# The second key block weighed with the third and fourth, a group later: two runs of 32-column matmuls a group instead of three

## What is computed

```python
x = x + 0.5 * ffn(layernorm(x))
x = x + attention(layernorm(x))
x = x + 0.5 * ffn(layernorm(x))

# attention, per sequence and head
q = x @ Wq;  latent = x @ Wkv_down            # latent: 32 channels
k = latent @ Wk_up;  v = latent @ Wv_up
p = softmax(where(causal, q @ k.T / 8, -inf))
y = p @ v;  out = y @ Wout                    # summed over the heads
```

## Time and profile before

| | us |
|---|---|
| runs | 913.27, 915.11, 913.05 |
| median | 913.27 |
| span of the profiled execution | 915.6 |
| TensorE matmul busy | 858.2 (94%) |
| GpSimd busy | 731.9 (80%) |
| VectorE busy | 644.4 (70%) |
| ScalarE busy | 549.3 (60%) |
| weight loads (beside the matmuls) | 572.1 (62%) |
| matmuls of L755, blocks 1 to 3 | 110.1, 1536 records |
| matmuls of L755, block 0 | 69.3, 512 records |

### The profile page before, as it was taken

The page is one execution under the profiler, slowest core; times in us unless marked ns, Lnnn a source line. Parts: engine busy times, 40 slices in busy tenths (PEclk is TensorE's granted clock), DMA queues, the critical chain, the costliest instruction groups (busy, mean ns, idle before and its releaser), DMA issues. The chain is left out here.

```text
span 915.6 us, 21654 instructions
## 1 busy us (share of the span) xinstructions
PE 858.2 (94%) x7750; PEld 572.1 (62%) x7750; DVE 644.4 (70%) x1818; ACT 549.3 (60%) x1113; POOL 731.9 (80%) x834
## 2 busy tenths in 40 slices
PE   5688999999999999999999999999999999999886
PEld 4455666666576666666566666666666666657455
DVE  3387577678767677768767777876867767776645
ACT  4444666757666565756756665766656575655551
POOL 4304789898989989898898989898988989789732
PEclk9878999999999999999999999999999999999999
DMA  4446251523535151533535152443525153340000
GB/s 101 113 111 140 54 118 36 124 73 85 124 82 126 42 129 39 120 88 82 126 71 130 33 126 57 98 110 82 125 58 119 37 117 74 83 102 14 14 24 12
DMA packets 77546, 77.89 MB, mean 85 GB/s; under 512 B 9392, under 2 KB 51136, under 8 KB 77440
## 3 DMA queue, kind: packets, MB, share of 16 engines
q1 hardware_dynamic: 76640, 75.45, 35.5%
q10 hardware_dynamic: 800, 1.07, 0.4%
HBM read 9.90 MB, written 8.39 MB: 20 GB/s over the span
## 5 line engine op out<-in xcount | busy, mean ns | idle before, releaser
L483 POOL TENSOR_TENSOR first_probs<-first_probs,later_probs 128x768 f32<-128x768 f32 x240 | 371.2, 1555 | 23.7 <-PE bank L755 23.7
L593 ACT ACTIVATE later_probs<-bank 128x384 f32<-128x384 f32 (+1 forms) x448 | 231.0, 538 | 153.5 <-PE bank L742 152.5
L742 PE MATMUL bank<-q_stack,keys 123*128 123x512 f32 (+1 forms) x704 | 308.4, 463 | 9.8 <-ACT first_probs L593 8.3
L1059 DVE TENSOR_REDUCE maxima<-bank 128x1 f32<-128x512 f32 (+1 forms) x384 | 254.9, 682 | 67.5 <-PE bank L811 67.3
L811 PE MATMUL bank<-keys,q_stack 122*128 122x512 f32 (+3 forms) x1024 | 256.3, 338 | 11.6 <-issue 2.8
L811 PEld LDWEIGHTS bank<-keys,q_stack 122*128 122x128 f32 x1024 | 181.8, 193 | 103.0 <-issue 41.4
L593 ACT ACTIVATE first_probs<-bank 128x512 f32<-128x512 f32 x256 | 139.9, 594 | 106.1 <-PE bank L742 102.2
L1059 DVE TENSOR_REDUCE block_max<-bank 128x4 f32<-128x512 f32 x256 | 173.6, 678 | 39.8 <-PE bank L811 39.1
L742 PEld LDWEIGHTS bank<-q_stack,keys 123*128 123x128 f32 x704 | 127.9, 191 | 72.0 <-ACT first_probs L593 33.7
L516 POOL TENSOR_SCALAR_AFFINE_SELECT later_probs<-later_probs 128x512 f32<-128x512 f32 x192 | 124.1, 647 | 55.5 <-ACT later_probs L593 55.5
L755 PE MATMUL bank<-later_probs,lat 128*32 128x384 f32 (+2 forms) x1536 | 110.1, 389 | 0.7 <-POOL later_probs L516 0.7
(11 more groups left out here) (127 smaller groups left out, 831.2 us busy)
## 6 DMA issues: line engine op xcount, KB each, us to landing
q_stack<-q_high SPq DMA_DIRECT2D x256, 128.0 KB, 2.4
q_stack<-q_low SPq DMA_DIRECT2D x128, 128.0 KB, 2.5
out_dram<-x SPq DMA_DIRECT2D x32, 256.0 KB, 2.6
x_in<-in_L_attn_x_bld_dram SPq DMA_DIRECT2D x16, 256.0 KB, 3.2
x_back<-out_dram SPq DMA_DIRECT2D x16, 256.0 KB, 3.0
keys<-keys_staged SPq DMA_DIRECT2D x15, 192.0 KB, 2.5
keys<-keys_staged SPq DMA_DIRECT2D x30, 96.0 KB, 2.4
lat<-lat_staged SPq DMA_DIRECT2D x16, 64.0 KB, 1.9
```

Of the source, the lines that this page charges most:

```text
L483: nc.gpsimd.tensor_tensor(total, total, later_probs[j - 1][:, heads], ALU.add).then_inc(added, 1)
L593: nc.scalar.activation(probs_of(s)[:, e:e + heads, 0:n], score_bank(t, u)[:, 0:heads * n].rearrange("p (e q) -> p e q", e=heads), ACT.Exp) ...
L742: nc.tensor.matmul(score_bank(t, u)[:, 0:heads * n], keys[par][:, PLAIN_BLOCK[j], :], q_stack[par][:, first:first + heads, j * P:L], start ...
L1059: nc.vector.tensor_reduce(out, seg, AX.X, ALU.max).then_inc(a_free, 1)
```

## The change

In a step with s % 4 = 1 the second block (j = 1) of the last group is weighed first, then the third and fourth; the step with s % 4 = 3 weighs nothing. Between its exponentials and its weighing a second block now lives until the next group's second block is being made, so `later_probs` for j = 1 gets a second buffer, chosen by the group's parity, and the exponential that writes it waits for the weighing and the sums of two groups ago instead of one. The order in which blocks are weighed stays. The last sequence keeps its tables. The number of matmuls, exponentials, masks and sums is the same.

```diff
-WEIGH = [[], [3, 2], [2], [2]]
+WEIGH = [[], [4, 3, 2], [2], []]
@@
-        later_probs = [sb(f"later_probs{j}", [P, HG, L - P * j]) for j in range(1, TT)]
+        later_probs = [[sb(f"later_probs{j}{i}", [P, HG, L - P * j]) for i in range(2 if j == 1 else 1)]
+                       for j in range(1, TT)]
@@
-            return later_probs[s % TT - 1] if s % TT else first_probs[s // TT % 2]
+            g, j = divmod(s, TT)
+            bufs = later_probs[j - 1] if j else first_probs
+            return bufs[g % len(bufs)]
@@
-                    nc.gpsimd.tensor_tensor(total, total, later_probs[j - 1][:, heads], ALU.add).then_inc(added, 1)
+                    nc.gpsimd.tensor_tensor(total, total, probs_of(g * TT + j)[:, heads], ALU.add).then_inc(added, 1)
@@
                     if e == 0:
-                        wait_batch(act, pv_done, t, 0, STEPS, s - TT + 1)
+                        ago = 2 if j == 1 else 1
+                        wait_batch(act, pv_done, t, 0, STEPS, s - ago * TT + 1)
                         if j in ADDED:
                             wait_batch(act, added, t, 0, PARTS * G * len(ADDED),
-                                       PARTS * ((g - 1) * len(ADDED) + ADDED.index(j) + 1))
+                                       PARTS * ((g - ago) * len(ADDED) + ADDED.index(j) + 1))
```

More of the change, by code:

```diff
@@ L1077, in last_adds @@
                             total = first_probs[g % 2][:, heads, j * P:L]
-                            nc.vector.tensor_tensor(total, total, later_probs[j - 1][:, heads], ALU.add).then_inc(added, 1)
+                            nc.vector.tensor_tensor(total, total, probs_of(g * TT + j)[:, heads], ALU.add).then_inc(added, 1)
                 def next_statistics():
```

## The result

The changed kernel takes 936.82 us (median of 4 runs, 936.49 to 937.52), the kernel before 914.19 in the same comparison (4 runs). The ratio is 1.0242, 95% interval 1.0217 to 1.0266: 22.6 us slower. The forecast was 934.4, in a range of 923 to 939.

The account below looks back on a forecast made before the run. TensorE sets the pace except where GpSimd's chain holds the projection and ScalarE covers savings. +1.52 us in thirteen rounds (+19.8), +0.67 and +0.7 in sequences 0 and 14 sum to +21.2: 934.4 us, range 923 to 939.

Parts of the forecast that it names:

- The two prices: TensorE's cost of weighing a second block: 0.88 us alone, 0.65 us beside the third and fourth blocks.
- Steps 3, 5 and 7: Two runs taken and one 0.65 us addition before the projection, hidden by GpSimd's chain: gain 0.
- The distance: From the score of step 2 to the first projection, ended by GpSimd's y_norm: fixed at 15.13 us.
- Steps 9, 13 and 1: Places where TensorE's longer run adds 0.65 us each, claimed to be paid whole.
- Step 11: Run removed before the front's query matmul, which waits for ScalarE's copy: only 0.26 of 0.88 us comes off.
- Step 15: Run removed before step 0, whose first exponential waits behind ScalarE's four tiles: gain 0.17 us; TensorE's wait about 1.1.
- third rival: One ScalarE cover, in step 11 or 15, gives way: 0.62 or 0.71 us a sequence back, about 926 us; chance 0.11.
- Sequence 0: First sequence, with no projection or tail before it, so steps 7 and 11 are gained: +0.67 us.
- Sequence 14: Sequence with no front beside it: bounded by -0.9 and +1.5 us, taken as +0.7.
- fourth rival: Step 5's longer run delays GpSimd: up to 0.65 us more in 13 sequences, 943 us; chance 0.06.
- TensorE's pace everywhere: Second rival: TensorE sets the pace all the way, each removed run worth 0.23 us, 899.5 us; chance 0.08.
- Both rivals with a cover giving way: ScalarE's covers in steps 11 and 15: one gives way, about 926 us, chance 0.11; both, some 917, chance 0.04.

Follow-up runs that it names:

- m1: Kernel before with one max unit a sequence taken out of step 10 and one more put into step 6; ratio 1.0052 over the kernel before.
- m3: Changed kernel with two more max units in steps 6 and 7, two in step 11, fewer in steps 12 to 14; ratio 1.0179 over the kernel before.

## Why the prediction was right

**The two prices.** 0.65 in company and 0.88 alone: the run of step 1 grew by 0.65, and the run of step 7 was worth 0.87. 60 x 0.23 = 13.8 us of work would go away by that; TensorE's busy time, whose ends are modelled, shows 9.9.

**Steps 3, 5 and 7 give nothing.** The distance is 15.14, forecast unchanged at 15.13. The wait before the projection grew to 0.70, forecast 0.6. The experiments with the cut sum show that the cause is GpSimd, not a coincidence. The slack that I claimed for step 5's longer run is there, 0.65 where I had 0.79; nothing was put between the exponential's end and the mask's start. One part is right without its reason. I wrote that steps 3 and 7 together take 0.88 + 0.88 and that TensorE arrives 0.88 - 0.65 = 0.23 earlier, which counts only one of the two; with both it would be 1.11 earlier, and the wait about 1.5. For sequence 0 I called step 3 hidden without saying behind what. The rows of step 4 give the reason: step 3's saving ends there, at VectorE's reduction and ScalarE's tiles, and TensorE's last max unit before the projection comes 13.81 us after the score of step 2 instead of 14.03, 0.22 earlier. The time doesn't depend on it.

**Steps 9, 13 and 1 are paid whole,** but for 0.05 of step 9's, which step 10 takes back. Group 1 moved alone costs 0.60 a round, with nothing gained at step 7.

**Step 11.** Forecast 0.26 off; 0.17 came at the query matmul, which starts 0.14 after the copy's end where I had allowed 0.05, and 0.20 at the score behind it. Its wait is 0.55, forecast 0.7. **Step 15.** Forecast 0.17 off; alone it leaves 0.65 - 0.47 = 0.18. The number is right, and ScalarE's tiles do end last there, as the cut shows. But of the 0.88 VectorE took the first 0.44, which the forecast didn't have, and so the sign named for it, a wait of 1.1, failed: it is 0.71. So the third rival's price of 0.71 for a cover that gives way here was too high: by the rows 0.26 would have come back, and the cut tiles gave 0.24.

**The round.** +1.52 forecast, +1.51 measured. Counted from the score of step 2 on, the changed kernel's scores are behind by 0.65 from the middle of step 5, by 0.01 at the projection, by 0.65 in step 9, 0.60 in step 11, 0.40 in step 12, 1.05 from step 13, 0.85 in step 1 of the next sequence and 1.50 at its end: each term in its place.

**The ends.** Sequence 0, given +0.67, has it: from the first score of the attention to the first projection the profiles take 71.46 us before and 72.08 after, +0.62. Sequence 14, given +0.7, costs about twice that, 1.3: I took a gain before its projection, which has no wait for GpSimd in the kernel before, but in the changed one step 5's 0.65 brought TensorE and GpSimd there later by 0.3 (13.98 us from the score of step 2, then 14.32). That is the fourth rival's path, in this one sequence. On the other side the profile of before holds two single delays, 0.85 in the first of the rounds of the earlier trace rows, by the wait for the keys, and 0.33 in the round of 52.30 us that ends at 721.24, and that of after holds none; and its first score comes 0.8 later (76.94, after 76.14), a start that differs by up to 3 us among all the profiles. So the spans differ by 19.8, and would differ by 21.8 without these. The medians differ by 22.6, by the ratio's interval between 19.8 and 24.3; the forecast was 21.2. That it is so near owes something to errors that cancel.

**The rivals.** TensorE's pace everywhere (899.5 us) falls with the four single groups. Both rivals with a cover giving way fall with the waits for ScalarE, which the cuts move. The fourth was open in sequence 14 alone, and in the ordinary rounds only after GpSimd had been relieved.

The Trainium skill, TensorEngine Tiling (Array Packing), Key Properties, has a change of tiling mode drain the engine. The rows agree as far as a run by itself costs more than the same block in company, 0.87 against 0.65 us. The time that would follow from these savings alone, 899.5 us, doesn't come, because in all four places most or all of what was taken went into waits for other engines.

## What to carry to other kernels

A saving on the busiest engine is worth what stands beside the place where it is saved: find for each place taken and each place given which wait ends next there, and add up those. A block of work that covers another engine's latency can be worth leaving where it is even if it runs dearer there: here moving it cost 1.51 us a round. Behind the cover that ends last a second one can stand, as VectorE's did in step 15; a forecast of the wait needs both, a forecast of the time only the last. When work moves between steps, look at the queue order of the engines that consume it: the step that gets rid of work can be the one that gets longer, as step 10 in m1.

## What was not expected of the hardware

With the run of step 3 moved alone (group 0), two single sequences were longer by about a microsecond. Stretches of one microsecond in step 4 of sequence 14, columns as in the earlier trace rows, the granted clock third from the right, and two rows in order of time:

```profile
813.00:814.00 1.00, 0.85 (x3) 0.30 (x2) 1.00 (x3) 0.68 (x2) 1.00 (x2) 1.00 0.99 207
814.00:815.00 1.00, 0.44 (x3) 0.44 (x3) 1.00 (x2) 0.51 (x1) 1.00 (x1) 1.00 0.26 60
...
817.00:818.00 1.00, 1.00 (x4) 0.56 (x2) 1.00 (x8) 0.52 (x1) 0.38 (x2) 0.50 0.00 0
818.00:819.00 1.00, 1.00 (x4) 0.84 (x4) 1.00 (x9) 0.74 (x3) 1.00 (x1) 0.50 0.00 0
...
817.24 0.63 PE L826 MATMUL bank<-keys,q_stack 122*128 122x512 f32 x1
817.67 0.63 PE L757 MATMUL bank<-q_stack,keys 123*128 123x512 f32 x1
```

In step 4, behind the thinned step 3, TensorE was busy for 0.44 us of one microsecond, waiting 0.68 for a reduction of VectorE, and 2 us later it was granted 0.50, that is 1.2 GHz, for some 3 us, in which the distance from one 512-column matmul to the next was 817.67 - 817.24 = 0.43 us, where it is 492.83 - 492.59 = 0.24 in the kernel before. The sequence took 1.3 us more than in the kernel before. The same stood in sequence 11 of that profile (0.63 in 660 to 664).

The other profiles tell more. Between the first projection and the last sequence such a fall stands in two others, behind step 4 as well: in the changed kernel with the cut sum (from 825.4, 0.53 us busy of one in 823 to 824) and in m3 (from 668.0, 0.32 of one in 665 to 666). Both have the thin step 3. It stands in none of the eight kernels with the full step 3, and not in the changed kernel or in its two with a ScalarE cut, where step 3 is as thin. So four falls in six profiles stand against none in eight, one execution each. At the start and in the last sequence every kernel has falls, the kernel before at 864.3 and 881.4. That the thinner step brings about the fall, and why not each time, was not tested; one of the ten launches of the group 0 kernel took 927.97 us at a mean granted clock of 0.937, the others 916.81 to 920.95 at 0.978 to 0.987.
